# Edge MLP of a four-layer graph network: every 64th tile fetched row by row by SP

## The chip, the cores and the metric

The kernel runs on one core of a Trainium2 chip. The metric is the device time of one execution in microseconds (us), as the median of the runs. The profile is of one execution, taken by the hardware profiler.

## The reference

Four graph layers run one after the other on the same 6250 nodes (128 features each) and 100000 edges, each followed by a residual and a layer norm. The change is in the third layer, the edge MLP:

```python
row, col = edge_index
e = concat([h[row], h[col]], axis=1)
e = silu(e @ We1 + be1)          # 64 wide
e = silu(e @ We2 + be2)
agg = segment_sum(e, row, num_segments=6250)
out = silu(concat([h, agg], axis=1) @ Wn1 + bn1) @ Wn2 + bn2
x = layernorm(x + h + out)
```

The fourth layer is two graph convolutions (GCN) over the same edges: `out = segment_sum((x @ W)[row] * norm, col) + b`.

## The kernel before

The program is a row of blocks. In each block every engine has its own code, and all engines meet at its end. The edges are sorted by the node that they are summed into and cut into 782 tiles of 128. Tiles go in groups of CG = 8, so there are 98 groups of tiles. The nodes are cut into blocks of 128; a step is one tile against one block of nodes, and as a tile can lie on two blocks there are 832 steps, which are 104 groups of 8 (CSTEP_GROUPS).

The block of the edge MLP starts at line 1973 and works so for each group of steps:

- SP loads the edges' positions in their node block, repeated over the 128 partitions, into one of two halves of `rel_rows` (L1998, 512 KB). One load serves two groups of steps. A load waits until DVE has used up the half that it overwrites (semaphore `l2_hotT`).
- POOL fetches the other end's table row of every edge: one indirect DMA (a gather) per tile, 128 rows of 64 floats from the table `table_edge_mlp` (`t2`) in HBM into one of 96 slots of `mlp_ring` (12 groups, CRING). The gathers of a group wait until ACT has placed their row numbers in `idx_now` (semaphore `l2_placed`), which it does as slots come free. POOL also counts: when all gathers of the group two back have landed, it raises `l2_landed` (the function `landed`).
- DVE makes a 0/1 matrix from `rel_rows` (L2116, `hotT`), PE multiplies the own node's half out of a table in SBUF with it (L2057), and DVE adds the fetched half out of `mlp_ring` (L2126, in `before_silu`, which waits for `l2_landed`). ACT applies silu (L2018), PE turns (L2067), ACT copies (L2023), PE multiplies by We2 (L2076), ACT applies silu (L2031) and places numbers for a later group (L2010, L2013), PE sums per node (L2088), and DVE adds the sum to `acc` (L2143) and clears the window (L2146).

DVE makes `hotT` three groups of steps ahead and adds the fetched half two ahead. The helper `conv_rounds` writes the first 12 groups out, then a loop over 12 groups, then the rest. SP's code is a loop of two loads.

In the two GCN blocks (function `convolution`) POOL gathers in the same way, but every 49th tile is fetched row by row: 64 rows by SP, 64 by ACT, each row a DMA of its own whose row number comes from a register. There are 15 such tiles in each block. This code is written out without a loop: registers are loaded 16 at a time from SBUF (L2359), and each row is a bounds step on the register (L2354) and the DMA with its address move (L2356). In a profile these are instructions of the queues SPq and ACTq.

Of the kernel before, what the change touches and what calls it, by code (L numbers as in the profile page):

```python
# [18 lines left out]
I32 = mybir.dt.int32  # L19
# [54 lines left out]
def place_lag(k):  # L74

    t = CG * k + CG - USED
    return CRING - 1 - k + (dense(t) // CG if t >= 0 else -1)
AW = 132
# [44 lines left out]
def build(nc, x, edge_i, edge_f, W_att_w, W_att_b, W1_w, W1_b, W2_w, W2_b, a_vec,  # L123
# [3 lines left out]
    with ctx:  # L127
# [43 lines left out]
        rel_rows = arena[:, LOOK2 + CSLOTS * EH:LOOK2 + CSLOTS * EH + 2 * CG * P].bitcast(BF16).rearrange("p (k e) -> p k e", k=2)  # L171
        src_t = sb("src_t", [P, COLS], I32)
# [107 lines left out]
        step2_need = tab_rows(CSTEP_GROUPS, 1).bitcast(I32)  # L280
        keep = NT * 3 * EH // 2
# [1364 lines left out]
        with nc.Block() as block:  # L1646
# [16 lines left out]
            def _(pe):  # L1663
# [11 lines left out]
         n2_xnT_kept, n2_e_mm, n2_e_kept, n2_e0, n2_e_rest, n2_e1, n2_split, n2_v, n2_factor, n2_rows, n2_bias) = (  # L1675
            sem(f"n2_{n}") for n in (
             "agg", "aggT", "aggT_kept", "o_mm", "o_kept", "xT", "xT_kept", "mm", "mixed", "var", "std", "factors", "xn", "xnT",
             "xnT_kept", "e_mm", "e_kept", "e0", "e_rest", "e1", "split", "vector", "factor", "rows", "bias"))
# [13 lines left out]
        with nc.Block() as block:  # L1692
            @block.vector
            def _(dve):
# [80 lines left out]
                dve.wait_ge(n2_rows, 48)  # L1775
                by_group = step2_node[:, 0:STEPS].rearrange("p (k u) -> p k u", u=CG)
# [191 lines left out]
        l2_landed, l2_clear = sem("l2_landed"), sem("l2_clear")  # L1968
# [4 lines left out]
        with nc.Block() as block:  # L1973
# [5 lines left out]
            def _(pool):  # L1979
                def step(i, g, k):  # L1980
                    pool.wait_ge(l2_placed, from_group(k, LAG))
                    landed(pool, i, g, k, l2_landed)
                    for u in range(CG):
                        slot = g * CG + u
                        if isinstance(k, int) and k == CTILE_GROUPS - 1 and u == CG // 2:
                            count_landed(pool, k - 1, l2_landed)
                        q_.indirect_dma_start(mlp_ring[:, slot * EH:(slot + 1) * EH], None, t2, bass.IndirectOffsetOnAxis(  # L1987
                            ap=idx_now[:, slot:slot + 1].bitcast(U32), axis=0)).then_inc(conv_gathered[g], 16)
# [3 lines left out]
                conv_rounds(pool, step, CTILE_GROUPS)  # L1992
                count_landed(pool, CTILE_GROUPS - 1, l2_landed)

            @block.sync
            def _(sp):
# [168 lines left out]
        for k in range(CTILE_GROUPS):  # L2165
            conv_count[k % CRING] += 16 * CG
# [581 lines left out]
```

## Time and profile before

| | |
|---|---|
| runs (3): median, lowest, highest | 7270.19, 7253.22, 7270.66 us |
| profiled execution: time, span of its instructions | 7208.03, 7206.1 us |
| busy share of the span: PE, DVE, ACT, POOL | 46%, 46%, 21%, 54% |
| edge MLP block: SP's first load to DVE's last add | 2982.2 to 4342.6 us |
| TensorE's mean granted clock over the span | 0.589 |

The profiled execution was 62 us faster than the median of the runs. Times in the trace are from the span's start. A row of a timeline gives the start, the length, the engine, the line, the operation and how many instructions were put together in it; in brackets stands how long the engine sat idle before, and what ended that.

### The profile page before, as it was taken

The page shows a single profiled execution, that of the slowest core. Times are in us where ns is not written, and L with a number is a line of the kernel's source. Part 1 is how long each engine was busy: PE and PEld are TensorE (multiplying, and loading weights), DVE is VectorE, ACT ScalarE, POOL GpSimd, SP SyncE. Part 2 cuts the span into 40 slices and gives each one's busy share as a digit, 9 for nine tenths or more (in the row PEclk, how much of TensorE's full clock was granted, in tenths as well). Part 3 has the DMA queues.
Part 4 walks back from the last instruction along what each step waited for, and adds up shares of the span by engine and source line. Part 5 has one row for each costly group of instructions (what it writes and reads, how often), then busy time and mean ns, then how long its engine had stood idle before and what let it go on. Part 6 is the DMA issues. An engine that isn't in the chain of part 4 may idle for free. (4 is left out here: it accounts for less than half of the span.)

```text
span 7206.1 us, 93020 instructions
## 1 busy us (share of the span) xinstructions
PE 3336.3 (46%) x16921; PEld 2837.8 (39%) x16922; DVE 3279.5 (46%) x11447; ACT 1487.5 (21%) x5629; POOL 3909.1 (54%) x4021
## 2 busy tenths in 40 slices
PE   4333333455555455577777785233333333333333
PEld 3233232444444444456656663222222322222223
DVE  6666666656656566433333344333333423333335
ACT  2333333344434343311111113000000000000001
POOL 5666666345655555356656532455555535555553
PEclk6555555577767766755555557555555565555555
DMA  4111112133333333111111111111111111111111
GB/s 112 44 43 44 43 43 46 45 103 97 103 96 96 95 98 93 31 41 42 42 41 39 40 34 37 35 42 41 39 40 40 35 41 41 40 39 39 41 41 45
DMA packets 230984, 386.34 MB, mean 54 GB/s; under 512 B 88844, under 2 KB 131689, under 8 KB 230653
## 3 DMA queue, kind: packets, MB, share of 16 engines
q0 software_dynamic: 141920, 294.25, 16.2%
q1 hardware_dynamic: 83900, 87.45, 4.0%
q14 instruction: 250, 2.04, 0.1%
q8 instruction: 82, 1.34, 0.1%
q10 hardware_dynamic: 4832, 1.25, 0.1%
HBM read 356.11 MB, written 26.56 MB: 53 GB/s over the span
## 5 line engine op out<-in xcount | busy, mean ns | idle before, releaser
L2378 POOL DMA_INDIRECT arena<-table_gcn,idx_now x1536 | 1459.0, 950 | 1418.6 <-ACT ew_now L2417 952.7
L2478 PE MATMUL pair<-arena,hotf 128*128 x3328 | 801.5, 422 | 1584.5 <-DVE hotf L2499 764.7
L2478 PEld LDWEIGHTS pair<-arena,hotf 128*128 128x128 f32 x3328 | 709.8, 316 | 1670.9 <-issue 1670.3
L2499 DVE TENSOR_SCALAR hotf<-iota,rel_now,ew_now 128x128 f32<-128x128 f32 x1664 | 442.4, 355 | 1769.2 <-ACT ew_now L2417 1303.3
L747 POOL DMA_INDIRECT arena<-table_key_value,idx_now x832 | 806.9, 970 | 612.5 <-ACT idx_now L735 364.7
L747 POOL DMA_INDIRECT arena<-table_attention,idx_now x816 | 830.2, 1017 | 443.3 <-issue 235.8
L1987 POOL DMA_INDIRECT arena<-table_edge_mlp,idx_now x784 | 755.4, 963 | 534.9 <-ACT rel_now L2013 311.8
L1203 PE MATMUL pair<-wide,hotf 128*128 128x130 f32 x1664 | 423.9, 435 | 857.1 <-ACT wide L1169 652.7
L1203 PEld LDWEIGHTS pair<-wide,hotf 128*128 128x128 f32 x1664 | 365.3, 323 | 918.3 <-ACT wide L1169 694.6
L1539 PE MATMUL pair<-wide,hotf 128*128 128x132 f32 x1664 | 349.1, 374 | 633.4 <-DVE acc L1569 440.6
L1539 PEld LDWEIGHTS pair<-wide,hotf 128*128 128x128 f32 x1664 | 300.4, 267 | 675.1 <-issue 673.9
L2412 ACT COPY idx_now<-src_t 128x8 int32<-128x8 int32 x192 | 36.0, 197 | 2304.7 <-issue 1575.8
L2088 PE MATMUL pair<-wide,hotf 128*128 128x64 f32 x1664 | 371.1, 409 | 28.2 <-issue 27.6
L2088 PEld LDWEIGHTS pair<-wide,hotf 128*128 128x128 f32 x1664 | 350.7, 316 | 39.2 <-issue 33.0
L1052 DVE TENSOR_TENSOR acc<-acc,pair 128x130 f32 x832 | 238.4, 287 | 209.4 <-remote 170.4
L2126 DVE TENSOR_TENSOR hot<-pair,arena 128x64 f32<-128x64 f32 x832 | 133.5, 225 | 435.0 <-remote 381.9
L1530 PE MATMUL pair<-arena 128*128 x1664 | 327.5, 363 | 8.7 <-issue 8.7
L1530 PEld LDWEIGHTS pair<-arena 128*128 128x128 f32 x1664 | 312.7, 279 | 9.2 <-issue 9.2
L1622 DVE TENSOR_REDUCE small<-pair 128x1 f32<-128x128 f32 x208 | 60.4, 291 | 513.1 <-remote 457.2
L2076 PE MATMUL pair<-we,tab 128*128 128x128 f32 x832 | 227.2, 428 | 126.9 <-issue 125.8
L2057 PE MATMUL pair<-arena,hotT 128*128 x2496 | 230.6, 237 | 116.5 <-issue 107.9
L1482 ACT ACTIVATE junk<-iota,rel_now 128x128 f32<-128x128 f32 x832 | 265.7, 390 | 16.0 <-issue 6.0
(378 smaller groups left out, 5989.3 us busy)
## 6 DMA issues: line engine op xcount, KB each, us to landing
arena<-table_gcn SPq DMA_DIRECT2D x1920, 0.5 KB
arena<-table_gcn ACTq DMA_DIRECT2D x1920, 0.5 KB
key<-rel_dram SPq DMA_DIRECT2D x104, 256.0 KB
arena<-rel_dram SPq DMA_DIRECT2D x52, 512.0 KB
arena<-table_gcn,idx_now POOLq DMA_INDIRECT x1536
arena<-table_key_value,idx_now POOLq DMA_INDIRECT x832
arena<-table_attention,idx_now POOLq DMA_INDIRECT x816
arena<-table_edge_mlp,idx_now POOLq DMA_INDIRECT x784
```

Source lines behind the costliest of these rows:

```text
L747: q_.indirect_dma_start(ring[:, slot, 0:width], None, table, bass.IndirectOffsetOnAxis(ap=idx_now[:, slot:slot + 1].bitcast(U32), axis=0)) ...
L1052: v.tensor_add(here, here, l0_bank(k, u)).then_inc(l0_acc[u], 1)
L1203: last = t_.matmul(l0_bank(k, u), hotf[:, g, u, :], wide[:, g, u, 0:D + 2], start=True, stop=True)
L1482: last = s_.activation(away[:, u * P:(u + 1) * P], iota[:, :], ACT.Abs, scale=-1.0, bias=rel_now[:, g * G + u:g * G + u + 1])
L1530: last = t_.matmul(QB[g % 2][:, u * P:(u + 1) * P], hotT_f[:, g, u * P:(u + 1) * P], flat(look[:, bass.ds(nodes[u], 1), :]), start=True, s ...
L1539: last = t_.matmul(bank[SUM + 2 * (g % 2) + u // 2][:, (u % 2) * AW:(u % 2 + 1) * AW], hotf[:, g, u, :], wide[:, g, u, :], start=True, sto ...
L1987: q_.indirect_dma_start(mlp_ring[:, slot * EH:(slot + 1) * EH], None, t2, bass.IndirectOffsetOnAxis(ap=idx_now[:, slot:slot + 1].bitcast(U ...
L2057: last = t_.matmul(LB[g % 2][:, u * EH:(u + 1) * EH], hotT8[:, g % 2, u * P:(u + 1) * P], flat(look2[:, bass.ds(node, 1), c * EH:(c + 1) * ...
L2088: last = t_.matmul(window[:, bass.ds(offset * EH, EH)], hot8[:, g % 2, u, :], s2[:, g % 2, u * EH:(u + 1) * EH], start=False, stop=(u == C ...
L2378: q_.indirect_dma_start(conv_ring[:, slot * D:(slot + 1) * D], None, table, bass.IndirectOffsetOnAxis(ap=idx_now[:, slot:slot + 1].bitcast ...
L2478: t_.matmul(sums[:, bass.ds(offset * D, D)], hot8[:, g % 2, u, :], conv_ring[:, bass.ds(slot * D, D)], start=False, stop=False)
L2499: last = v.tensor_scalar(out=hot8[:, g % 2, u, :], in0=iota[:, :], scalar1=rel_now[:, at], scalar2=ew_now[:, at], op0=ALU.is_equal, op1=AL ...
```

## The change

SP fetches the first tile of every eighth group of tiles (groups 8, 16, ... 96, so 12 tiles in all) row by row into one of three buffers, `mlp_lone`, and copies the buffer to the tile's slot in `mlp_ring` with one more DMA. POOL fetches the other 772 tiles; where it counts a group with such a tile it waits for that copy too (`l2_lone_out`). The row numbers are loaded at the start of the block before, as sorted keys, and DVE cuts them down to 13 bits there. SP's loads, which were a loop, are now written out with the rows between them: after each of the loads 1 to 48 stand 32 rows, and after the loads 5, 9, ... 49 the copy of the tile before. POOL's code is written out over 24 groups instead of 12, as is its loop's body.

```diff
+MLP_EVERY = 8
+MLP_LONE = (CTILE_GROUPS - 1) // MLP_EVERY
+MLP_BUFFERS = 3
...
                 dve.wait_ge(n2_rows, 48)
+                dve.wait_ge(n2_lone, 32)
+                for rows in lone_rows:
+                    v.tensor_scalar(out=rows, in0=rows, scalar1=(1 << KEY_BITS) - 1, scalar2=None, op0=ALU.bitwise_and)
...
+                of_lone = sorted_dram[0:(MLP_LONE + 1) * MLP_EVERY * CG, :].bitcast(I32).rearrange("(one n r) e -> one n r e", one=1, r=MLP_EVERY * CG)
+                for rows, first, end in ((lone_rows[0], 1, 1 + LONE_KEYS), (lone_rows[1], 1 + LONE_KEYS, 1 + MLP_LONE)):
+                    sp.dma_start(rows.rearrange("one (n e) -> one n e", e=P), of_lone[:, first:end, 0, :]).then_inc(n2_lone, 16)
...
+                    pool.wait_ge(conv_gathered[h], m * per + ((q // CRING + 1) * 16 * CG - 16 * alone + conv_count[h] - back * per))
+                    if q % MLP_EVERY == 0 and (q or not isinstance(m, int) or m):
+                        assert not back
+                        pool.wait_ge(l2_lone_out, m * (16 * both // MLP_EVERY) + 16 * (q // MLP_EVERY))
+                    pool.sem_inc(l2_landed, 1)
...
-                    for u in range(CG):
+                    for u in range(1 if q % MLP_EVERY == 0 and not (isinstance(k, int) and k == 0) else 0, CG):
...
-                for n in range(2):
-                    rows(2 * n, n)
-                with sp.Fori(1, CSTEP_GROUPS // 4) as i:
-                    for n in range(2):
-                        sp.wait_ge(l2_hotT, i * 4 + 2 * n - 2)
-                        rows(i * 4 + 2 * n, n)
+                regs = [sp.alloc_register(f"l2_sp_row{u}") for u in range(ROW_REGS)]
+                per_load = P * 2 // MLP_EVERY
+
+                def lone_part(n, first, end):
+                    for p in range(first, end):
+                        if p % ROW_REGS == 0:
+                            at = (n - 1) % LONE_KEYS * P + p
+                            sp.reg_load(regs, lone_rows[(n - 1) // LONE_KEYS][0:1, at:at + ROW_REGS])
+                        row = sp.snap(regs[p % ROW_REGS], min_val=0, max_val=NP - 1)
+                        sp.dma_start(mlp_lone[p:p + 1, n % MLP_BUFFERS, :], t2[bass.ds(row, 1), :]).then_inc(l2_lone_in, 16)
+
+                def lone_placed(n):
+                    k = n * MLP_EVERY
+                    sp.wait_ge(l2_lone_in, 16 * P * n)
+                    sp.wait_ge(l2_placed, from_group(k, LAG))
+                    slot = k % CRING * CG
+                    sp.dma_start(mlp_ring[:, slot * EH:(slot + 1) * EH], mlp_lone[:, n % MLP_BUFFERS, :]).then_inc(l2_lone_out, 16)
+
+                for load in range(CSTEP_GROUPS // 2):
+                    if load >= 2:
+                        sp.wait_ge(l2_hotT, 2 * load - 2)
+                    rows(2 * load, load % 2)
+                    if load % 4 == 1 and 1 <= load // 4 <= MLP_LONE:
+                        lone_placed(load // 4)
+                    n, part_of = (load + 3) // 4, (load + 3) % 4
+                    if 1 <= n <= MLP_LONE:
+                        if part_of == 0 and n > MLP_BUFFERS:
+                            sp.wait_ge(l2_landed, (n - MLP_BUFFERS) * MLP_EVERY + 1)
+                        lone_part(n, part_of * per_load, (part_of + 1) * per_load)
```

On SP, the edge MLP block before is these instructions (L1998 is the load of `rel_rows`, twice ahead of the loop and twice in its body):

```order
L1995 UNCONDITIONAL_BRANCH
L1998 DMA arena<-rel_dram 128x2048 x2
L2002 UNCONDITIONAL_BRANCH
L2002 ISA
L1998 ISA
L1998 DMA arena<-rel_dram 128x2048
L1998 ISA
L1998 DMA arena<-rel_dram 128x2048
L2002 REGISTER_ALU
L2002 COMPARE_AND_BRANCH
```

The same engine with the change, where load 5 stands in the middle of the block (L2034 is the load, L2052 the copy to the ring, L2043 the load of 16 registers, L2044 and L2045 a row's bounds step and its DMA):

```order
L2045 DMA arena<-table_edge_mlp 1x64
L2034 DMA arena<-rel_dram 128x2048
L2052 DMA arena<-arena 128x64
L2043 TENSOR_LOAD key
L2044 ISA
L2045 DMA arena<-table_edge_mlp 1x64
```

Between one load and the next there now stand 32 pairs of L2044 and L2045 and two register loads; SP's whole program grows from 4061 such rows to 7284.

POOL in the same block before, from its first gather to the loop's first gathers:

```order
L1978 UNCONDITIONAL_BRANCH
L1987 DMA arena<-table_edge_mlp,idx_now 128x64 x96
L1935 UNCONDITIONAL_BRANCH
L1935 ISA
L1951 REGISTER_ALU
L1987 DMA arena<-table_edge_mlp,idx_now 128x64 x8
```

And with the change:

```order
L1990 UNCONDITIONAL_BRANCH
L2017 DMA arena<-table_edge_mlp,idx_now 128x64 x190
L2024 UNCONDITIONAL_BRANCH
L2024 ISA
L2000 REGISTER_ALU
L2017 DMA arena<-table_edge_mlp,idx_now 128x64 x7
```

Of 24 groups ahead of the loop two have lost their first gather, and the loop's first group has seven.

## Rows read from the trace of the kernel before

**Rows 1.** Busy time in the edge MLP and the first GCN block (stages view).

```profile
core 0: us, PE busy (x) PEld busy (x) DVE busy (x) ACT busy (x) POOL busy (x), PEclk, DMA share, GB/s
2982.00:4343.00 1361.00, 981.82 (x5617) 810.67 (x5618) 455.37 (x1976) 200.29 (x519) 755.38 (x784) 0.52 0.16 40
4425.00:5557.00 1132.00, 358.82 (x1642) 303.77 (x1642) 350.08 (x838) 32.52 (x246) 622.13 (x657) 0.55 0.15 39
```

**Rows 2.** Waits in the edge MLP block: in total, times, longest.

```profile
POOL arena L1987 <- ACT rel_now L2013: 311.8, 70, 22.9
POOL arena L1987 <- issue: 221.9, 710, 4.1
PEld pair L2076 <- issue: 190.9, 206, 3.2
```

**Rows 3.** Waits of SP's queue in the edge MLP block.

```profile
SPq L1998 <- DVE hotT L2116: 568.2, 24, 35.4
```

**Rows 4.** SP's loads in the edge MLP: timeline, last three, and length in ns.

```profile
2982.24 1305.31 SPq L1998 DMA_DIRECT2D arena<-rel_dram  x52
...
4253.63 33.92 SPq L1998 DMA_DIRECT2D arena<-rel_dram  x3
...
L1998 SPq DMA_DIRECT2D arena<-rel_dram x52: 332/337/426, 2982.2 to 4287.2; - x52
```

**Rows 5.** PE: two neighbouring turns of the edge MLP's loop (timeline).

```profile
3372.35 1.09 PE L2067 MATMUL pair<-ident,junk 128*128 128x128 f32 x4
...
3383.26 0.45 PE L2067 MATMUL pair<-ident,junk 128*128 128x128 f32 x1 [0.30 <-ACT junk L2018]
```

**Rows 6.** POOL's gathers in the edge MLP: min/median/max ns, and one in the timeline.

```profile
L1987 POOL DMA_INDIRECT arena<-table_edge_mlp,idx_now x784: 938/944/1467, 2984.4 to 4250.9; - x196
...
2988.37 0.94 POOL L1987 DMA_INDIRECT arena<-table_edge_mlp,idx_now  x1 [0.30 <-issue]
```

**Rows 7.** DVE at the end of the block before the edge MLP (timeline).

```profile
2980.97 1.00 DVE L1777 TENSOR_TENSOR tab<-tab 1x832 int32<-1x832 int32 x1
```

**Rows 8.** SP's rows in the two GCN blocks (timeline of SP).

```profile
4425.78 1131.26 SPq L2356 DMA_DIRECT2D arena<-table_gcn  x960
...
5822.69 1120.39 SPq L2356 DMA_DIRECT2D arena<-table_gcn  x960
```

**Rows 9.** SP's waits for its rows to land in both GCN blocks.

```profile
SPq L2406 <- DMA arena<-table_gcn: 20.7, 20, 1.3
```

**Rows 10.** Instructions of one row: min/median/max ns (source views).

```profile
L2356 SPq MOVE arena<-table_gcn x1920: 3/29/1406, 4425.7 to 6942.4; - x192
L2356 SPq DMA_DIRECT2D arena<-table_gcn x1920: 3/225/788, 4425.8 to 6942.4; - x192
...
L2354 SPq FUSED_REGOPS  x1920: 2/44/1392, 4425.6 to 6941.7; - x192
...
L2359 SPq TENSOR_LOAD <-tab x120: 4/1137/1394, 4424.4 to 6933.5; - x120
```

**Rows 11.** SP's first and second tile of rows in the first GCN block.

```profile
4425.78 85.87 SPq L2356 DMA_DIRECT2D arena<-table_gcn  x64
...
4513.99 42.78 SPq L2356 DMA_DIRECT2D arena<-table_gcn  x64
```

**Rows 12.** DVE: the first hotT, hotT 98, all 104, and the last adds.

```profile
2986.18 1.07 DVE L2116 TENSOR_SCALAR hotT<-arena,part 128x1024 bf16<-128x1024 bf16 x2 [2.73 <-DMA arena<-rel_dram]
...
4278.14 0.41 DVE L2116 TENSOR_SCALAR hotT<-arena,part 128x1024 bf16<-128x1024 bf16 x1
...
L2116 DVE TENSOR_SCALAR hotT<-arena,part x104: 414/415/681, 2986.2 to 4320.6; 128x1024 bf16<-128x1024 bf16 x104
...
L2143 DVE TENSOR_TENSOR acc<-acc,pair x104: 671/687/690, 3072.5 to 4341.9; 128x512 f32 x104
```

**Rows 13.** ACT's rows after SP's last row in the second GCN block (timeline).

```profile
6978.12 5.42 ACTq L2356 DMA_DIRECT2D arena<-table_gcn  x10
...
6984.27 17.65 ACTq L2356 DMA_DIRECT2D arena<-table_gcn  x12
```

More of the change, by code:

```diff
@@ L171, in build @@
         rel_rows = arena[:, LOOK2 + CSLOTS * EH:LOOK2 + CSLOTS * EH + 2 * CG * P].bitcast(BF16).rearrange("p (k e) -> p k e", k=2)
+        mlp_lone = arena[:, LOOK2 + CSLOTS * EH + 2 * CG * P:LOOK2 + CSLOTS * EH + 2 * CG * P + MLP_BUFFERS * EH].rearrange("p (n c) -> p n c", c=EH)
         src_t = sb("src_t", [P, COLS], I32)
@@ L280, in build @@
         step2_need = tab_rows(CSTEP_GROUPS, 1).bitcast(I32)
+        LONE_KEYS = SORT // P
+        lone_rows = [key[0:1, :].bitcast(I32), tab_rows((MLP_LONE - LONE_KEYS) * P, 1).bitcast(I32)]
         keep = NT * 3 * EH // 2
@@ L1674, in build @@
         (n2_agg, n2_aggT, n2_aggT_kept, n2_o_mm, n2_o_kept, n2_xT, n2_xT_kept, n2_mm, n2_mixed, n2_var, n2_std, n2_factors, n2_xn, n2_xnT,
-         n2_xnT_kept, n2_e_mm, n2_e_kept, n2_e0, n2_e_rest, n2_e1, n2_split, n2_v, n2_factor, n2_rows, n2_bias) = (
+         n2_xnT_kept, n2_e_mm, n2_e_kept, n2_e0, n2_e_rest, n2_e1, n2_split, n2_v, n2_factor, n2_rows, n2_bias, n2_lone) = (
             sem(f"n2_{n}") for n in (
              "agg", "aggT", "aggT_kept", "o_mm", "o_kept", "xT", "xT_kept", "mm", "mixed", "var", "std", "factors", "xn", "xnT",
-             "xnT_kept", "e_mm", "e_kept", "e0", "e_rest", "e1", "split", "vector", "factor", "rows", "bias"))
+             "xnT_kept", "e_mm", "e_kept", "e0", "e_rest", "e1", "split", "vector", "factor", "rows", "bias", "lone"))
         t2_out = [sem(f"n2_t2_out{n}") for n in range(2)]
@@ L1966, in at_least @@
                 eng.wait_ge(signal, k + more)
-        l2_landed, l2_clear = sem("l2_landed"), sem("l2_clear")
+        l2_landed, l2_clear, l2_lone_in, l2_lone_out = (sem(f"l2_{n}") for n in ("landed", "clear", "lone_in", "lone_out"))
         (l2_placed, l2_hotT, l2_look, l2_pre, l2_s1, l2_s1T, l2_s1T_kept, l2_e, l2_s2, l2_same, l2_sum, l2_acc) = (
@@ L1979, in _, with wait_rows, step @@
             def _(pool):
-                def step(i, g, k):
-                    pool.wait_ge(l2_placed, from_group(k, LAG))
-                    landed(pool, i, g, k, l2_landed)
-                    for u in range(CG):
+                both = 2 * CRING
+                assert both % MLP_EVERY == 0 and CRING % (both // MLP_EVERY + 1) == 0
+                def wait_rows(m, q, back=0):
+                    h = q % CRING
+                    alone = sum(1 for k in range(1, q + 1) if k % MLP_EVERY == 0 and k % CRING == h)
+                    per = 32 * CG - (16 if any(k % MLP_EVERY == 0 and k % CRING == h for k in range(1, both + 1)) else 0)
+                    pool.wait_ge(conv_gathered[h], m * per + ((q // CRING + 1) * 16 * CG - 16 * alone + conv_count[h] - back * per))
[3 more added lines that the diff above has]
+                    pool.sem_inc(l2_landed, 1)
+                def step(m, q):
+                    k, g = m * both + q, q % CRING
+                    pool.wait_ge(l2_placed, from_group(k, LAG))
+                    if isinstance(k, int) and k < 2:
+                        pool.sem_inc(rounds, 1)
+                    else:
+                        wait_rows(m, (q - 2) % both, 0 if q >= 2 else 1)
+                    for u in range(1 if q % MLP_EVERY == 0 and not (isinstance(k, int) and k == 0) else 0, CG):
                         slot = g * CG + u
                         if isinstance(k, int) and k == CTILE_GROUPS - 1 and u == CG // 2:
-                            count_landed(pool, k - 1, l2_landed)
+                            wait_rows((k - 1) // both, (k - 1) % both)
                         q_.indirect_dma_start(mlp_ring[:, slot * EH:(slot + 1) * EH], None, t2, bass.IndirectOffsetOnAxis(
@@ L1991, in _ @@
                 pool.wait_ge(t2_out[1], 16 * (NB // 2))
-                conv_rounds(pool, step, CTILE_GROUPS)
-                count_landed(pool, CTILE_GROUPS - 1, l2_landed)
+                for q in range(both):
+                    step(0, q)
+                with pool.Fori(1, CTILE_GROUPS // both) as m:
+                    for q in range(both):
+                        step(m, q)
+                for k in range(CTILE_GROUPS // both * both, CTILE_GROUPS):
+                    step(k // both, k % both)
+                wait_rows((CTILE_GROUPS - 1) // both, (CTILE_GROUPS - 1) % both)
             @block.sync
@@ L2165, in build @@
         for k in range(CTILE_GROUPS):
-            conv_count[k % CRING] += 16 * CG
+            conv_count[k % CRING] += 16 * (CG - 1 if k and k % MLP_EVERY == 0 else CG)
         (n3_xT, n3_sumT, n3_xT_kept, n3_sumT_kept, n3_h_mm, n3_h_kept, n3_mm, n3_mixed, n3_stats, n3_std, n3_factors, n3_xn,
```

## Prediction

> **What bounds the kernel now.** I read the stages view first, to see which stretch the change can reach: the edge MLP block lasts 1361 us, and in it PE works 982 us, POOL 755, DVE 455 [rows 1]. PE comes nearest to full, at a granted clock of 0.52. Then the waits of that block. POOL sits idle 311.8 us in 70 waits for ACT to place row numbers, that is, for free slots [rows 2]; the other 221.9 us are 710 gaps of 0.3 us between gathers, which belong to a gather's price. So POOL is ahead of the others for most of the block. SP is further from the edge still: its queue waits 568.2 us in all for DVE to use up `rel_rows`, at most 35.4 us at once [rows 3], and each of its 52 loads costs it 0.34 us [rows 4]. What sets the pace is the circle of PE, ACT and DVE: one turn of PE's loop takes 3383.26 - 3372.35 = 10.9 us where nothing is late [rows 5], against 1361 / 104 = 13.1 us on average. Much of the difference is PE's own stalls before instructions that wait for nothing in the profile ("issue", 190.9 us at one of its lines) [rows 2]. The reader should keep one number: two groups of steps, the distance between two loads of SP, last 1305.31 / 51 = 25.6 us [rows 4].
>
> **The change, part by part.**
>
> *POOL loses 12 gathers.* One is 0.94 us and 0.30 us of gap, 1.24 us together [rows 6]; 12 are 15 us. POOL waits 20 times that long for ACT, so I take 0. The bounds are 0 and 15 us gained. Writing its code out further adds no gather; I take 0 for it too, since the gap stays 0.30 us at 710 of 784 gathers.
>
> *DVE gets two operations on one partition, 1024 and 512 numbers long.* The nearest row is the subtraction of 832 numbers on one partition, 1.00 us, the last thing DVE does there [rows 7]. By length the two make 1.85 us. The edge MLP block starts at 2982.24, right after that row, so I count all of it: +1.8 us. If the last write of the table still ends later, it is 0. SP's two loads of numbers at that block's start lie ahead of waits for DVE: 0.
>
> *SP gets 1536 rows* (12 tiles of 128), 62 loads and copies up to load 49, and 96 register loads. This is the term that decides. The block of before has no such row, but both GCN blocks do: the same three instructions per row and the same register load per 16, written out in the same way. There SP takes 1131.26 us for 960 rows in the first block and 1120.39 us in the second [rows 8], 1.178 and 1.167 us per row, waits for landed rows included; those waits are only 20.7 us over both blocks [rows 9], so SP is not held up by its DMAs. By their medians the instructions of a row take 44 + 29 + 225 ns, and the register load 1137 / 16 = 71 ns more, 0.37 us in all [rows 10]. The rest is time in which an instruction comes late: maxima of 1.4 us stand beside medians of 29 and 44 ns in the same rows. The pace is not even: the first tile took 85.87 us for 64 rows (1.34 us per row), the second 42.78 (0.67) [rows 11].
>
> I take SP's average, 1.172 us, because 1920 rows of the same code made it. Between two loads then lie 32 x 1.172 + 0.34 = 37.8 us, against the 25.6 us that two groups of steps need now. SP's 568 us of slack are used up and SP becomes the pace: `hotT` of groups 2L and 2L+1 cannot be made before load L, which stands behind 32 rows.
>
> Rows: 1536 x 1.172 = 1800 us. 50 loads (0 to 49) and 12 copies at 0.34 us: 21 us. Load 49 is then issued at 2982.2 + 1.8 + 1800 + 21 = 4805. From a load to its `hotT` are 2986.18 - 2982.24 = 3.9 us. From `hotT` 98 to the end of the last add lie 4341.9 + 0.7 - 4278.1 = 64.5 us now [rows 12], in turns of 8.5 us (`hotT` 103 follows at 4320.6, so five turns take 42.5 us) [rows 12]; at the 10.9 us of the loop [rows 5] they would be 14 us more, and I take 75. The block ends at about 4805 + 4 + 75 = 4884 instead of 4342.6: +541 us.
>
> *The waits that come with it.* POOL's wait for the copy stands ahead of group 8n+2, and behind it are all its later gathers and the count `l2_landed`, for which DVE's add of the fetched half (L2126) waits. SP places a tile every four loads, 151 us; POOL's 63 gathers between are 78 us, so POOL catches up and adds nothing to SP's pace. The copy itself waits for slots, which are long free when SP is last. The GCN blocks behind start later by the same 541 us and are otherwise untouched.
>
> Sum: 541 us on the profiled execution's 7208 us is 7749 us. The median of the runs is 62 us above that execution, so I add the sum to the median: 7270 + 541 = 7811 us.
>
> A page of the Trainium skill speaks against this term: "Runtime: NRT & Kernel Launch", section "Instruction fetch mechanics", says that a sequencer loads the next block of straight code while it works on the current one, so that this is mostly hidden, and that code written out is better off than code with branches. By that rule a row would cost its instructions alone and the kernel would keep its time; the trace does not agree, with 1.17 us per row against 0.37. What the mechanism would do here is the first rival.
>
> **Rivals.**
>
> *SP stays hidden (not slower).* Load 49 left at 4253.6 before [rows 4]. SP keeps to that if a row takes less than (4253.6 - 2982.2 - 21) / 1536 = 0.81 us; below that pace the rows fall into SP's present waits. For it: the second tile's 0.67 us [rows 11], the medians' 0.37 us, and that ACT does not issue rows in this block, as it does beside SP in the GCN. Against it: SP's average over 30 tiles, and ACT's rows after SP had finished: 22 rows in 5.42 + 17.65 us, still 1.05 us each [rows 13]. The rule just named from the Trainium skill is this case. Time: 7270 + 2, or down to 7257 if POOL's 15 us count: about 7268. Chance 0.11.
>
> *The rows come slower still.* PE's loop has its own late instructions in this block [rows 2], and SP's written-out code comes on top. At the first tile's 1.34 us: 1536 x 1.342 = 2061 us, 261 more than above, 8072 us. For it: PE does 5617 matmuls here against 1642 in a GCN block [rows 1]. Against it: only the first tile was that slow. Chance 0.08 for a pace above 1.3.
>
> *POOL is the pace after all.* DVE's add would be released earlier wherever a group has seven gathers. 311.8 us of waits for ACT speak against it, and the most it gives is 15 us, 7255. To be faster by over 22 us something more would have to shrink. Chance 0.02.
>
> **How the numbers follow.** 0.3% of 7270 is 22 us, about what a measurement of this kernel can tell from no change. The forecast, SP as the pace with a row between 0.95 and 1.3 us, has 0.79. At ACT's 1.05 us it gives 7811 - 188 = 7623; at 0.95 us 1536 x 0.222 = 341 less, 7470; at 1.295 us 189 more, 8000. So the range is 7470 to 8000, which leaves out 0.13 below (hidden or faster) and 0.08 above. Slower 0.87, same 0.11, faster 0.02.
>
> **What would show it.** Right: SP's timeline over the block is solid row DMAs of 32 between loads about 38 us apart, SP's wait for `hotT` nearly gone, DVE idle ahead of its `hotT` until the load lands, and a block of some 1900 us. The GCN blocks keep their 1131 and 1120 us. The term is wrong where the pitch of SP's rows differs from 1.17 us; the mechanism is wrong if SP still waits for DVE by hundreds of microseconds, or if POOL waits for the copy while loads are on time.

## The result and the profile after

| | before | with the change |
|---|---|---|
| median of the runs (lowest to highest) | 7261.70 us (7251.90 to 7270.66, 4 runs) | 7518.39 us (7506.23 to 7543.93, 4 runs) |
| ratio of the runs, 95% interval | 1 | 1.0359 [1.0333, 1.0385] |
| profiled execution: time, span | 7208.03, 7206.1 us | 7523.81, 7521.9 us |
| edge MLP, SP's first load to DVE's last add | 1360.4 us | 1659.4 us |

The kernel is 257 us slower by its medians. The two traces differ by 316 us, because the profiled execution of before lies 54 us under its median and that of after 5 us above. Of the 316 us, 299 are in the edge MLP; the other 17 are ahead of it, and nearly all of them in blocks that the change leaves as they were (the trace is 18.7 us behind that of before already at 1477 us). The GCN blocks, with the same code, have their old length (1397.8 us from SP's first row in the first to that in the second, after 1396.9). So the place is the one forecast; the size is about half.

The stages view of the block answers to [rows 1]: each engine is about as busy as before, in 300 us more.

```profile
core 0: us, PE busy (x) PEld busy (x) DVE busy (x) ACT busy (x) POOL busy (x), PEclk, DMA share, GB/s
2999.00:4660.00 1661.00, 990.39 (x5617) 827.13 (x5618) 460.82 (x1977) 203.50 (x519) 732.97 (x772) 0.52 0.14 33
```

SP's queue, which waited 568.2 us for `hotT` [rows 3], now waits for next to nothing (its waits between its first load and its last):

```profile
SPq L2052 <- DMA arena<-table_edge_mlp: 5.7, 12, 0.5
SPq L2034 <- DVE hotT L2175: 0.2, 1, 0.2
```

DVE in its turn waits for SP's loads, which it hardly did before (2.7 us, once), and POOL has a second wait beside that for ACT [rows 2], the one for the copied tile. Two of PE's lines show late starts that end no wait ("issue") of 283.8 and 272.4 us; the same lines had 107.9 and 27.6 us before. The waits of the block after:

```profile
DVE hotT L2175 <- DMA arena<-rel_dram: 340.5, 46, 25.5
POOL arena L2017 <- ACT rel_now L2072: 316.5, 40, 35.6
POOL arena L2017 <- DMA arena<-arena: 299.6, 9, 41.0
PE pair L2116 <- issue: 283.8, 166, 5.4
PE pair L2147 <- issue: 272.4, 151, 3.2
```

The timeline of SP shows what it does: 32 rows, a load, 32 rows, a load, with no wait to speak of. But 32 rows take 53.7, 33.8, 19.4 and 14.6 us in turn, and much the same for the other tiles:

```profile
3280.72 0.51 SPq L2052 DMA_DIRECT2D arena<-arena  x1
3282.86 53.68 SPq L2045 DMA_DIRECT2D arena<-table_edge_mlp  x32
3336.59 0.45 SPq L2034 DMA_DIRECT2D arena<-rel_dram  x1
3339.18 33.80 SPq L2045 DMA_DIRECT2D arena<-table_edge_mlp  x32
3373.02 0.36 SPq L2034 DMA_DIRECT2D arena<-rel_dram  x1
3374.77 19.41 SPq L2045 DMA_DIRECT2D arena<-table_edge_mlp  x32
3394.22 0.36 SPq L2034 DMA_DIRECT2D arena<-rel_dram  x1
3395.98 14.55 SPq L2045 DMA_DIRECT2D arena<-table_edge_mlp  x32
3410.58 0.35 SPq L2034 DMA_DIRECT2D arena<-rel_dram  x1
3411.47 0.49 SPq L2052 DMA_DIRECT2D arena<-arena  x1
```

All 1536 rows lie between 3002.3 and 4583.0 (source view, min/median/max ns; the GCN's rows stand under them and answer to [rows 8]): 1.029 us per row, loads and copies included, where 1.172 was forecast for a row alone. Their instructions have the medians of [rows 10].

```profile
L2045 SPq MOVE arena<-table_edge_mlp x1536: 2/29/1395, 3002.2 to 4583.0; - x192
L2045 SPq DMA_DIRECT2D arena<-table_edge_mlp x1536: 3/228/1399, 3002.3 to 4583.0; - x192
...
4743.11 1127.65 SPq L2415 DMA_DIRECT2D arena<-table_gcn  x960
6140.88 1102.21 SPq L2415 DMA_DIRECT2D arena<-table_gcn  x960
```

### The profile page after: what moved, and what is told of

It reads as the page before. It is cut to its first block and busy times, and to the rows that moved or that the text cites. A ratio compares the mean times of both kernels' runs of the same rounds, so it can differ in the third digit from the quotient of the medians.

```text
span 7521.9 us, 97587 instructions
## 1 busy us (share of the span) xinstructions
PE 3382.2 (45%) x16921; PEld 2892.1 (38%) x16922; DVE 3286.8 (44%) x11449; ACT 1492.1 (20%) x5629; POOL 3880.2 (52%) x4009
## 3 DMA queue, kind: packets, MB, share of 16 engines
q8 instruction: 82, 1.34, 0.1%
q10 hardware_dynamic: 4832, 1.25, 0.1%
## 5 line engine op out<-in xcount | busy, mean ns | idle before, releaser
L2017 POOL DMA_INDIRECT arena<-table_edge_mlp,idx_now x772 | 733.0, 949 | 881.3 <-ACT rel_now L2072 316.5
L1209 PEld LDWEIGHTS pair<-wide,hotf 128*128 128x128 f32 x1664 | 367.1, 324 | 935.3 <-ACT wide L1175 649.0
L1545 PE MATMUL pair<-wide,hotf 128*128 128x132 f32 x1664 | 375.4, 395 | 597.5 <-DVE acc L1575 407.3
L1545 PEld LDWEIGHTS pair<-wide,hotf 128*128 128x128 f32 x1664 | 324.4, 287 | 641.6 <-issue 639.4
L2147 PE MATMUL pair<-wide,hotf 128*128 128x64 f32 x1664 | 384.4, 404 | 272.8 <-issue 272.4
L2147 PEld LDWEIGHTS pair<-wide,hotf 128*128 128x128 f32 x1664 | 363.9, 318 | 275.2 <-issue 268.8
L2116 PE MATMUL pair<-arena,hotT 128*128 x2496 | 254.8, 236 | 332.7 <-issue 283.8
L2116 PEld LDWEIGHTS pair<-arena,hotT 128*128 128x128 bf16 x2496 | 208.4, 122 | 383.4 <-issue 354.5
L1536 PE MATMUL pair<-arena 128*128 x1664 | 345.1, 378 | 8.6 <-DVE arena L1592 8.6
L1536 PEld LDWEIGHTS pair<-arena 128*128 128x128 f32 x1664 | 330.3, 293 | 9.2 <-issue 9.0
```

Of the source, the lines that this page charges most:

```text
L1209: last = t_.matmul(l0_bank(k, u), hotf[:, g, u, :], wide[:, g, u, 0:D + 2], start=True, stop=True)
L1536: last = t_.matmul(QB[g % 2][:, u * P:(u + 1) * P], hotT_f[:, g, u * P:(u + 1) * P], flat(look[:, bass.ds(nodes[u], 1), :]), start=True, s ...
L1545: last = t_.matmul(bank[SUM + 2 * (g % 2) + u // 2][:, (u % 2) * AW:(u % 2 + 1) * AW], hotf[:, g, u, :], wide[:, g, u, :], start=True, sto ...
L2116: last = t_.matmul(LB[g % 2][:, u * EH:(u + 1) * EH], hotT8[:, g % 2, u * P:(u + 1) * P], flat(look2[:, bass.ds(node, 1), c * EH:(c + 1) * ...
L2147: last = t_.matmul(window[:, bass.ds(offset * EH, EH)], hot8[:, g % 2, u, :], s2[:, g % 2, u * EH:(u + 1) * EH], start=False, stop=(u == C ...
```

## The experiments

They ran on five chips, on which the kernel before took 7184 to 7270 us by its medians; every ratio is to the kernel before on the same chip. Line numbers shift a little from kernel to kernel.

**1. Rows with constant addresses** (e_static). This kernel fetches rows 0 to 1535 of the table, not the edges' rows.

```diff
-                        if p % ROW_REGS == 0:
-                            at = (n - 1) % LONE_KEYS * P + p
-                            sp.reg_load(regs, lone_rows[(n - 1) // LONE_KEYS][0:1, at:at + ROW_REGS])
-                        row = sp.snap(regs[p % ROW_REGS], min_val=0, max_val=NP - 1)
-                        sp.dma_start(mlp_lone[p:p + 1, n % MLP_BUFFERS, :], t2[bass.ds(row, 1), :]).then_inc(l2_lone_in, 16)
+                        row = (n - 1) * P + p
+                        sp.dma_start(mlp_lone[p:p + 1, n % MLP_BUFFERS, :], t2[row:row + 1, :]).then_inc(l2_lone_in, 16)
```

Expected: 

> Every row DMA of SP gets a constant address (other rows than the edges ask for), so a row is one instruction instead of three and the 96 register loads are gone; the number, size and place of the DMAs stay. Theory A (SP sets the pace because its instructions come late, in number): a row costs about a third, 1536 rows some 500 to 700 us, which fits into SP's old slack: 7250 to 7290 us. Rival B (the small DMA itself costs SP about 1 us): the rows stay near 1.03 us and the time at 7500 to 7540 us.

**2. Half of the rows** (e_half). 64 rows of each tile come one by one, the other 64 as one DMA of neighbouring rows (not the edges' rows).

```diff
-                per_load = P * 2 // MLP_EVERY
+                per_load = P // MLP_EVERY
...
+                        if part_of == 3:
+                            sp.dma_start(mlp_lone[P // 2:P, n % MLP_BUFFERS, :], t2[n * P:n * P + P // 2, :]).then_inc(l2_lone_in, 16)
```

Expected: 

> SP fetches 64 of a tile's 128 rows one by one, 16 after each load; the other 64 come with one DMA of 64 neighbouring rows (other rows than asked for). Copy, POOL's waits and POOL's code as with the change. Theory A (SP's occupancy by rows is the whole cost): 768 rows at 1.0 to 1.2 us are 770 to 920 us, less than the 1271 us that SP has until load 49, so 7250 to 7300 us. Rival C (the wait of POOL for the copy, or the longer code of POOL, costs by itself): 7400 us or more.

Measured: 1.0042 [1.0016, 1.0068] and 1.0028 [1.0004, 1.0052]. SP waits for `hotT` again in both, e_static first:

```profile
SPq L2034 <- DVE hotT L2172: 562.5, 41, 23.5
```

```profile
SPq L2034 <- DVE hotT L2177: 486.2, 46, 21.1
```

So it is the number of SP's instructions that costs, not the 1536 DMAs (e_static has them all), and once SP has time left what remains of the change costs 0.3 to 0.4%.

**3. All rows ahead of the first load** (e_front), while next to nothing else runs in the block.

```diff
+                for n in range(1, MLP_LONE + 1):
+                    lone_part(n, 0, P)
                 for load in range(CSTEP_GROUPS // 2):
...
-                        lone_part(n, part_of * per_load, (part_of + 1) * per_load)
```

Expected: 

> All 1536 rows are issued ahead of load 0, into twelve buffers, while PE, DVE and ACT wait for load 0 and POOL makes its first 48 gathers and then waits. The loads then follow with nothing between. Theory D (a row is slow while POOL gathers, about 1.55 us, and quick while it does not, about 0.6): some 60 us slow, the rest at 0.45 to 0.6 us, in all 700 to 950 us; total 7960 to 8220 us. Rival E (the price of a row is its own, 1.03 us): 1580 us of rows, total about 8840 us. Rival F (PE's loop is what slows SP): as D, since PE waits too.

**4. The same, with 16 x 48 further gathers by POOL beside the rows** (e_front_pool).

```diff
+                for r in range(16):
+                    for slot in range(48):
+                        q_.indirect_dma_start(mlp_ring[:, slot * EH:(slot + 1) * EH], None, t2, bass.IndirectOffsetOnAxis(
+                            ap=idx_now[:, slot:slot + 1].bitcast(U32), axis=0)).then_inc(l2_extra, 16)
+                    pool.wait_ge(l2_extra, 16 * 48 * (r + 1))
```

Expected: 

> As the run with all rows ahead of load 0, and POOL makes 16 times 48 additional gathers into the ring at the same time, some 980 us of gathering, before its own; PE, DVE and ACT still wait. Theory D (gathers slow the rows): SP makes only some 640 rows in these 980 us, and the remaining 900 in 400 to 540 us: rows take about 1400 to 1500 us, with a pace of about 1.5 us and then about 0.5. Rival F (PE's loop slows the rows): rows take about 700 us, as without the gathers, and the gathers alone set the start of the block.

Measured (one execution each): 7959.57 and 8879.22 us. In e_front 1536 rows take 822 us; behind the first 128, which had gathers beside them, a row takes 0.504 us. In e_front_pool a row takes 4.2 us nearly throughout the extra gathers, across POOL's short pauses too: an address move (MOVE), 29 ns by its median in [rows 10], takes 699 ns at the least and 700 by its median, and each instruction starts 1.4 us after the last one. Timeline of e_front, then the source view of e_front_pool from 3100 to 3400 us:

```profile
2974.29 821.99 SPq L2045 DMA_DIRECT2D arena<-table_edge_mlp  x1536
```

```profile
L2051 SPq MOVE arena<-table_edge_mlp x70: 699/700/709, 3100.7 to 3396.1; - x70
L2051 SPq DMA_DIRECT2D arena<-table_edge_mlp x70: 699/704/709, 3102.1 to 3397.5; - x70
```

PE, DVE and ACT were waiting in both, so PE's loop has no part in it. POOL's gathers do, and more than I had expected (rows for 1770 us, where 1400 to 1500 were forecast).

**5. The rows of the last one in a loop** (e_front_pool_loop): is it that new code comes late?

```diff
+                for part in range(2):
+                    for first in range(0, P, ROW_REGS):
+                        with sp.Fori(0, min(MLP_LONE - part * LONE_KEYS, LONE_KEYS)) as n:
+                            sp.reg_load(regs, lone_rows[part][0:1, bass.ds(n * P + first, ROW_REGS)])
+                            for p in range(first, first + ROW_REGS):
+                                row = sp.snap(regs[p % ROW_REGS], min_val=0, max_val=NP - 1)
```

Expected: 

> As the kernel with all rows in front and 16 x 48 further gathers of POOL beside them, but SP's rows of a group of 16 partitions stand in a loop over the tiles (8 passes, then 4), so that the same 47 or so instructions are run 8 and 4 times; the same number of instructions is executed, and every row is the one asked for. Theory G (what is late beside the gathers is the bringing of SP's next instructions, which lie in a straight piece of code run once): only the first pass of each loop pays, so a row is some 0.5 us in the later passes and the 1536 rows take 900 to 1900 us in all, with the extra gathers still running when they end. Rival H (SP carries out its instructions slowly beside gathers, whether their code is new or not): some 4 us per row in every pass while POOL gathers, and rows until 1770 us after their start as before.

**6. A shorter loop for PE** (e_pe4, and e_after_pe4 on the changed kernel): 4 groups in the body instead of 12.

```diff
-                conv_rounds(pe, step, CSTEP_GROUPS)
+                for g in range(4):
+                    step(0, g, g)
+                with pe.Fori(1, CSTEP_GROUPS // 4 - 1) as i:
+                    for g in range(4):
+                        step(i, g, i * 4 + g)
+                for k in range(CSTEP_GROUPS - 4, CSTEP_GROUPS):
+                    step(k // 4, k % 4, k)
```

Expected: 

> The kernel before, with TensorE's part of the edge MLP written as a loop of 4 groups instead of 12 (24 passes, the first and last four groups written out): the same matmuls with the same operands. Theory G, if it holds for TensorE too: the late starts without a wait that the trace of before charges to TensorE in this block (PEld L2076 190.9 us, PE L2076 107.9 us and others) shrink to under a half, and the whole is 1 to 3% faster. Rival I (these late starts are TensorE's own register loads and waits, not the bringing of code): within 0.3% of before, with the same late starts.

Expected of the second: 

> The changed kernel with TensorE's loop of the edge MLP cut to 4 groups in the same way. Rows by SP set the pace of this block in the changed kernel, at a pace that goes by how much of the time POOL gathers. If so, a quicker TensorE gives little or nothing back: ratio to the kernel before 1.025 to 1.040. Were TensorE's late starts (PE L2116 283.8 us) the cause of the longer block, it would come back to 1.00 or below.

Measured: the loop takes 9437.75 us, more than without it, and its rows take 4.29 us while POOL gathers and 0.78 behind that. The first pass is no dearer than the later ones. PE's shorter loop gives 0.999 [0.9965, 1.0015], on the changed kernel 1.039 [1.0358, 1.0422]: nothing, and PE's late starts at L2076 stay (130.9 us after 125.8). What theory G forecast, that only new code comes late, did not come true. Little code was moved besides: in the trace of e_front_pool, from 3000 to 3400 us, the queue of instructions moved 5 packets (queue, kind: packets, MB, share of the DMA engines). Whether the instructions of an engine come late by some other way than new code, these runs don't tell.

```profile
q0 software_dynamic: 9706, 9.95, 13.0%
q1 hardware_dynamic: 192, 0.02, 0.0%
q14 instruction: 5, 0.04, 0.0%
```

**7. Rows that nobody uses** (e_unused). POOL gathers all 784 tiles by the code of before; the 1536 rows stay in their buffers.

```diff
-                    sp.dma_start(mlp_ring[:, slot * EH:(slot + 1) * EH], mlp_lone[:, n % MLP_BUFFERS, :]).then_inc(l2_lone_out, 16)
...
-                        pool.wait_ge(l2_lone_out, m * (16 * both // MLP_EVERY) + 16 * (q // MLP_EVERY))
```

Expected: 

> The changed kernel, but POOL fetches all 784 edge tiles as before the change, in the code of before, and the rows that SP fetches one by one are copied nowhere and used by nothing; there is no wait for a copy. Theory A (SP is busy with the rows and sends its loads of the step rows late): as slow as the change, ratio 1.03 to 1.05. Rival C (what costs is that POOL waits for the copied tile): 1.00 to 1.01.

Measured: 1.0147 [1.0109, 1.0185], between the two theories. SP is the pace here too (one wait of 8.6 us for `hotT`; DVE waits 629.2 us for its loads), but a row takes 0.90 us instead of 1.03, beside 12 gathers more. So the price of a row is no matter of the number of gathers. I sorted SP's rows by how long POOL's unbroken run of gathers (a burst: no gap over 0.6 us) had lasted when a row started, by the starts in the trace; a cell holds rows x mean us from a row to the next:

```
                  no gather     0-5 us       5-10 us      10-15 us    over 15 us
GCN of before     913 x 0.61    621 x 0.89   233 x 2.34   69 x 3.89   81 x 3.93
change           1012 x 0.58    294 x 0.95   104 x 2.10   41 x 3.26   82 x 4.23
unused rows       728 x 0.60    552 x 0.83   236 x 1.75    5 x 3.37   14 x 4.00
```

The columns hold roughly in these three kernels, and ACT's own rows, which run beside SP's in the GCN alone, leave no clear mark in them. They do not hold everywhere: in the kernel of pairs with unused rows (experiment 9) the last two are 112 x 2.34 and 83 x 2.96. In the change 123 rows take 41 x 3.26 + 82 x 4.23 = 481 of the 1581 us. With unused rows a burst is mostly one group, 8 gathers in 10 us; in the change POOL stops for the copy and then gathers up to 32 in 40 us.

That is not SP's trouble alone. One such burst of the change, 3154.3 to 3194.1, by windows: PE starts 13 and 35 products in the first two stretches of 5 us, then 2, 2 and 7 in the last 29.8 us. Under it stand SP's row instructions of the first and the fifth stretch: 6 rows in 5 us, 5 in 19.8.

```profile
3154.30:3159.30 5.00, 3.46 (x13) 2.59 (x13) 4.30 (x20) 1.22 (x2) 3.87 (x4) 0.50 0.12 20
3159.30:3164.30 5.00, 4.84 (x35) 4.52 (x34) 2.37 (x13) 1.31 (x4) 3.78 (x4) 0.50 0.15 31
3164.30:3169.30 5.00, 0.42 (x2) 0.21 (x2) 0.00 (x0) 0.00 (x0) 3.77 (x4) 0.50 0.15 27
3169.30:3174.30 5.00, 0.42 (x2) 0.21 (x2) 0.00 (x0) 0.00 (x0) 3.78 (x4) 0.50 0.14 26
3174.30:3194.10 19.80, 2.12 (x7) 1.14 (x8) 0.00 (x0) 0.00 (x0) 15.11 (x16) 0.50 0.15 27
3194.10:3202.70 8.60, 4.46 (x18) 3.70 (x17) 2.99 (x13) 1.54 (x5) 0.04 (x1) 0.50 0.02 5
...
L2045 SPq DMA_DIRECT2D arena<-table_edge_mlp x6: 17/228/717, 3154.3 to 3157.9; - x6
...
L2045 SPq DMA_DIRECT2D arena<-table_edge_mlp x5: 691/691/724, 3175.7 to 3193.2; - x5
```

The kernel before does the same in its bursts of two groups, without any row of SP. One of them, in halves: 59 products, then 8.

```profile
3292.50:3302.50 10.00, 9.20 (x59) 7.93 (x59) 3.17 (x18) 1.89 (x5) 7.75 (x8) 0.50 0.13 25
3302.50:3312.50 10.00, 2.78 (x8) 1.86 (x8) 1.50 (x3) 0.00 (x0) 7.57 (x8) 0.50 0.26 79
```

**8. Copies two loads earlier** (e_early): POOL need not stop for them, all else is the change.

```diff
-                    if load % 4 == 1 and 1 <= load // 4 <= MLP_LONE:
-                        lone_placed(load // 4)
-                    n, part_of = (load + 3) // 4, (load + 3) % 4
+                    if load % 4 == 3 and 1 <= (load + 1) // 4 <= MLP_LONE:
+                        lone_placed((load + 1) // 4)
+                    if load == 0:
+                        lone_part(1, 0, per_load)
+                    n, part_of = (load + 5) // 4, (load + 5) % 4
```

Expected: 

> The changed kernel with SP's rows of every tile two loads earlier, and so the copy to the ring as well (behind load 4n - 1 instead of 4n + 1; the first 64 rows stand behind loads 0); nothing else differs. Theory K (the wait for the copy is the dearer half: behind it POOL gathers in bursts of up to 60 us, and SP's rows grow dearer the longer a burst lasts, from 0.95 us in its first 5 us to 4.2 us from 15 us on; the same 1536 rows between bursts of 10 us cost 0.86 us each): POOL's wait for the copy goes from 299.6 us to under 60, its bursts to 10 us, the rows to 0.83 to 0.92 us each, and the ratio to 1.01 to 1.025. Rival L (the number of rows and of gathers alone sets it): rows at 1.0 us and 1.03 to 1.04 as the change.

Measured: 1.0130 [1.0100, 1.0159]. The rows take 1356 us, 0.88 each, the mean burst 10.3 us instead of 18.7. POOL's wait for the copy is gone; among the longest waits of the block POOL's is again that for ACT:

```profile
DVE hotT L2177 <- DMA arena<-rel_dram: 723.2, 48, 85.8
POOL arena L2017 <- ACT rel_now L2074: 440.4, 91, 41.4
```

**9. POOL's groups in pairs**, with unused rows (e_unused_pairs) and, as a control, in the kernel before (e_before_pairs).

```diff
-                    pool.wait_ge(l2_placed, from_group(k, LAG))
+                    if g % 2 == 0:
+                        pool.wait_ge(l2_placed, from_group(k + 1, LAG))
```

Expected: 

> As the kernel whose rows are used by nothing and whose POOL gathers all 784 tiles (1.0147), but POOL waits for the place of two groups at once and then gathers 16 tiles in one burst of 20 us instead of 8 in one of 10. Rows, gathers and everything else are the same in number; no copy and no wait for one. Theory K: by the pace of a row against the time since the burst began (0.95 us in the first 5 us, some 2.0 in the next 5, some 3.7 behind that, 0.5 with no gather) a cycle of 28.2 us holds 5 / 0.95 + 5 / 2.0 + 10 / 3.7 + 8.2 / 0.5 = 27 rows, 1.05 us each, so the 1536 rows take 1610 us and the ratio is 1.035 to 1.05. Rival L (the number of rows and of gathers alone sets it): rows at 0.86 us and 1.01 to 1.02 as without the pairs.

Expected of the control: 

> A control: the kernel before, without any row fetched by SP in this block, with POOL waiting for the place of two groups at once and gathering 16 tiles in one burst, as in the kernel of pairs with unused rows. If the pairs cost through SP's rows alone (theory K), 1.00, at most 1.005. If gathering in pairs costs by itself (theory M: every second group of tiles starts one group later, and VectorE, which waits for tiles 381.9 us in the trace of before, waits longer), it is 1.01 to 1.035, and the slowdown of the kernel of pairs with unused rows (1.0333 against 1.0147) says nothing of the price of a row.

Measured: 1.0333 [1.0304, 1.0363], a little under theory K's range, the rows at 1.01 us; but the control, with no row at all, is at 1.0210 [1.0184, 1.0236]. Pairs cost without SP's rows. Either late tiles do it (M), or bursts of 20 us slow PE as in the windows above; these two runs alone don't tell.

The control's trace also shows an engine that a burst does not slow. One burst of 16 gathers runs there from 3333.3 to 3353.0. DVE comes out of a wait of 12.5 us when the burst is 16.4 us old, and makes its next 16 operations in 3 us; PE, which has worked all through the burst, starts three products in about the same time (timelines of DVE and PE, 3348.9 to 3353.0).

```profile
3349.71 1.28 DVE L2127 TENSOR_TENSOR hot<-pair,arena 128x64 f32<-128x64 f32 x8 [12.49 <-remote]
3350.91 1.79 DVE L2134 TENSOR_SCALAR hotf<-iota,rel_now 128x128 f32<-128x128 f32 x8
...
3348.95 0.21 PE L2058 MATMUL pair<-arena,hotT 128*128 x1 [1.85 <-issue]
3349.66 0.21 PE L2058 MATMUL pair<-arena,hotT 128*128 x1 [0.50 <-issue]
3351.81 0.21 PE L2058 MATMUL pair<-arena,hotT 128*128 x1 [1.94 <-issue]
```

DVE does so 41 times in this block (idle for 4 us or more, then at work later than 10 us in a burst): some 30 instructions, 0.1 us from one to the next. So a late point in the burst is not enough to slow an engine: PE, which has been at work in the burst, is slowed, DVE after its wait is not.

**10. POOL waits for its own gathers after every group** (e_before_drain in the edge MLP of the kernel before, e_conv_drain in its convolutions too, e_after_drain in the edge MLP of the change). The wait can only hold a gather back, and a burst ends after 8 gathers, at 9.7 us in the median.

```diff
+        def drained(pool, i, g, k):
+
+            if not isinstance(k, int) or k >= 1:
+                pool.wait_ge(conv_gathered[(g - 1) % CRING], conv_count[(g - 1) % CRING] + 16 * CG * (i + (1 if g else 0)))
...
+                    drained(pool, i, g, k)
                     pool.wait_ge(l2_placed, from_group(k, LAG))
```

Expected of e_before_drain: 

> The kernel before, except that in the edge MLP POOL waits, ahead of every group, until the 8 gathers of its group before have landed: the same gathers, none in advance, so a burst is 8 gathers (10 us) with a pause of some 2 us or more behind it, where before it is often 16 (20 us). Theory K, wider (late in a burst of gathers the other engines' instructions start some 1.4 us apart, TensorE's too: in the trace of before one product follows another after 0.18 us in the first 10 us of a burst, after 0.9 to 1.6 us behind that): TensorE's late starts without a wait (PEld L2076 190.9 us, PE L2076 125.8 us, L2057 107.9 us) fall to under a half, and the whole is 0.5 to 2% faster although POOL waits more. Rival M (tiles that come later are what costs): 1.005 to 1.03, as the kernel of before in pairs (1.021).

Expected of e_conv_drain: 

> As the one before it, with the same wait of POOL in both GCN convolutions too, where SP and ScalarE fetch rows one by one and POOL's bursts are 17.6 us in the mean. Theory K, wider: rows by SP and ScalarE at 0.85 us or less instead of 1.13 to 1.18, TensorE's late starts (PEld L2478 1670 us) down by a third or more, and the whole 3 to 10% faster than before. Rival M: slower than before by 1 to 4%, since POOL's 768 gathers of each convolution get 96 pauses more.

Expected of e_after_drain: 

> The changed kernel with the same wait of POOL in the edge MLP alone; the copies stand where they stood, and POOL is still held by them. Theory K: no burst over 10 us of gathers, rows at 0.75 to 0.9 us each instead of 1.03, ratio to before 1.00 to 1.02. Rival L or M (the hold at the copies and the later tiles are what costs): 1.035 to 1.06, since POOL waits yet more.

Measured: 0.9786 [0.9760, 0.9812], 0.9332 [0.9305, 0.9358] (6785.71 us against 7270.44) and 1.0115 [1.0091, 1.0140]. M's forecasts fell: all three are faster than without the wait. Contrary to my expectation POOL did not wait more in the end: in the block of e_before_drain, 1262.8 us long by its trace instead of 1360.4, it is idle for 518 us instead of 605. The block accounts for 98 of the 147 us between the medians; where the rest lies the traces don't show. PE's late starts at its product with We2, 125.8 us before, fall to 24.3, those of the weight loads there from 190.9 [rows 2] to 74.0, while those at its first product stay (120.8 after 107.9). The three together are 219.1 us after 424.6, not under the half that was forecast. PE's waits in the block, first of before, then of e_before_drain:

```profile
PE pair L2076 <- issue: 125.8, 107, 3.1
PE pair L2057 <- issue: 107.9, 102, 3.9
```

```profile
PE pair L2063 <- issue: 120.8, 168, 3.8
PE pair L2082 <- issue: 24.3, 35, 1.6
PEld pair L2082 <- issue: 74.0, 140, 1.6
```

In e_after_drain the rows take 3016.9 to 4431.1, 0.92 each, a little over the forecast. In e_conv_drain a convolution lasts 5583.50 - 4356.29 = 1227 us from SP's first row to that of the next, where it was 5822.69 - 4425.78 = 1397 [rows 8]. SP's rows got hardly cheaper, against my expectation of 0.85 us: 1112.68 / 960 = 1.16 us. POOL now gathers for most of the time (768 gathers in 1184 us instead of 1289), so fewer of them fall where nothing gathers. With SP's rows 19 us quicker and the convolution 170, the gain is not in SP's rows. It goes along with ACT's 960 rows of the same tiles: from the first to the last they take 5383.7 - 4357.4 = 1026 us instead of 5606.5 - 4426.9 = 1180, which is 153 us less. PE's late starts without a wait at its weight loads in the convolutions, forecast to fall by a third or more, fell from 1670.3 to 1555.5 us only, so that part of the expectation failed. Why ACT's rows gain and SP's don't was not taken apart. SP's rows of e_conv_drain, then ACT's of the first convolution before (L2356) and there (L2362):

```profile
4356.29 1112.68 SPq L2362 DMA_DIRECT2D arena<-table_gcn  x960
...
5583.50 1077.14 SPq L2362 DMA_DIRECT2D arena<-table_gcn  x960
...
L2356 ACTq DMA_DIRECT2D arena<-table_gcn x960: 3/225/1407, 4426.9 to 5606.5; - x192
...
L2362 ACTq DMA_DIRECT2D arena<-table_gcn x960: 3/231/1392, 4357.4 to 5383.7; - x192
```

## Why the prediction was right in sign and wrong in size

**The mechanism was right in the main.** SP's 568 us of slack were used up, SP became the pace, DVE waited for its loads, and nothing behind the block moved. Experiments 1 and 2 show it from the other side: give SP time and the cost goes. The end of the block came as worked out: 76.4 us from SP's last row to the last add, against 4 + 75. (One slip there has no weight: by the prediction's own numbers five turns of 10.9 us instead of 8.5 are 12 us more, not 14.)

**The step that failed is the size of the row term**: "I take SP's average, 1.172 us, because 1920 rows of the same code made it." The code was the same, its surroundings were not. Rows and loads took 4583.0 - 3000.0 = 1583 us where 1821 were forecast: 238 of the 242 us by which the block came out shorter than forecast (299 us longer than before instead of 541). From 299 to the measured 257 it is 17 us more ahead of the block, hardly any of them the change's (DVE's two operations, 1.8 us in the forecast, took 0.67 and 0.41), and 59 us less because the two profiled executions lie differently to their medians: the sum was made in one trace and added to a median. A row has no price of its own: it is 0.5 to 0.6 us while POOL gathers nothing, and up to 4.2 us late in a burst (3, 4 and the table of 7). In the GCN 48% of the rows fell where nothing gathered, here 66% (913 of 1917, 1012 of 1533). The two tiles at 1.34 and 0.67 us [rows 11] stood there as a warning that an average hid two paces.

**"POOL catches up and adds nothing to SP's pace" was wrong too**, and in the other direction. Held by the copy, POOL catches up in bursts of up to 40 us, and those make the rows dear; with the copies earlier the change costs 1.3% instead of 3.6%. So two errors stood against each other: the rows are cheaper than in the GCN because POOL idles more here, and dearer than they need be because POOL is stopped and released.

**The rivals.** "SP stays hidden" set its threshold at 0.81 us per row; the kernels at 0.88 to 0.92 us (7, 8 and e_after_drain) cost 1.2 to 1.5%, the one at 1.03 costs 3.6%. That is in keeping with the threshold, which none of them reached; no run tried a pace just under it. "The rows come slower still" named PE's loop as the cause; PE has no part in it (3, 4). "POOL is the pace" did not come.

**The page on instruction fetch** was set against a trace that does not settle it. "Runtime: NRT & Kernel Launch", section "Instruction fetch mechanics", of the Trainium skill says that fetch of straight code is mostly hidden; I set 1.17 us per row against it. No run here contradicts the page: the rows came no quicker in a loop than as straight code (4.29 us), and 5 packets of instructions were moved in 400 us. Late instructions are not by themselves late code.

**What stays open.** That the instructions of an engine that works on beside POOL's gathers come later the longer the gathers go on is shown for SP and PE by rows, windows and the runs with shorter bursts; why they do, and why it settles at 1.4 us, no run here shows. DVE after a wait is not slowed at first (9); whether it is the work an engine has done in the burst that counts, or something else, no run puts to the test. All runs here recorded spans and clock, so whether the pace is the same with nothing recorded isn't shown either. How the 2.1% of the control in pairs splits between late tiles and slowed engines was not taken apart.

## What to carry to other kernels

Before you take a price from another block, sort its instances by what ran beside them; where the minimum and the median of an instruction are tiny and its maximum is a round figure (29 and 1400 ns here), the price may be the neighbour's. Here the neighbour was POOL's unbroken gathers: a wait that cut them into groups of 8 made the kernel before 6.7% faster (e_conv_drain, the fastest kernel of this study), while 12 gathers fewer, paid for with 1536 rows of three instructions on SP, made it 3.6% slower. A wait that stops an engine and then releases it in a burst can cost more at the engines beside it than at its own.

## What the runs showed of the hardware that was not expected

- Late in a run of indirect gathers by POOL (pitch 1.25 us in the kernel before, 1.40 in experiment 5), an instruction of SP, which never pauses there, starts 1.4 us after the one before it, a register step as well as a DMA; a row of three takes 4.2 us. With no gather it is 0.50 us.
- It sets in by degrees: 0.83 to 0.95 us per row in the first 5 us of a burst, 1.75 to 2.3 in the next 5, over 3 behind that in the three kernels of the table (2.3 to 3.0 in the kernel of pairs).
- It reaches PE too: 59 products in the first 10 us of a burst, 8 in the next 10. In the kernel before 331 of the 1360 us of the edge MLP lie later than 10 us in a burst, and PE starts some 280 of its 5617 products there. DVE, coming out of a wait at such a point, runs some 30 instructions 0.1 us apart.
- A pause of 2.4 us behind every 8 gathers keeps the rows at 0.92 us (median of the pauses in e_after_drain; 2.35 us in e_before_drain). Pauses of 1.7 to 3.3 us between the longer runs of experiment 4, most of them of 28 to 48 gathers, change nothing: SP goes on at 4.2 us per row across them.
